# A two-layer transformer kernel: FFN result copied out of PSUM before it is normalized, recurrence weights loaded early, and the router run one chunk ahead of the shared expert

## The chip, the cores and the metric

The kernel runs on one core of a Trainium2 chip. The metric is the device time of one execution in microseconds. TensorE (PE in the profile) multiplies, VectorE (DVE), ScalarE (ACT) and GpSimd (POOL) do the elementwise work, SyncE (SP) issues most transfers. All engines execute their own instruction lists strictly in order and wait for each other on counting semaphores.

## The reference, cut to what matters

Two layers on 2048 tokens of width 512, each an attention-like part and an FFN part, with a layer norm ahead of each part and a residual around it.

```python
x = x + attention(ln(x))
x = x + fp4_ffn(ln(x))        # h = silu(gate) * up ; y = h @ w_down.T ; y / rms(y)
x = x + recurrence(ln(x))     # state = d*state + (1-d)*(x @ W_in.T) ; state @ W_out.T + bias
x = x + moe(ln(x))            # softmax router, top 6 of 64 experts, at most 128 tokens each,
                              # plus a shared expert (gs * us) @ sh_down.T of inner width 704
```

## The kernel before, in words

The 16 token tiles of 128 tokens live in SBUF as `x_residual` for the whole kernel. Work goes in four chunks of 512 tokens (four tiles each). Six phases follow each other, with a barrier of all engines between two of them; the change touches three: `ffn_phase`, `recurrence_phase` and `router_phase`. Every product is made of high and low float parts, so each operand is split (a copy that rounds, `..._hi`, on ScalarE, and a subtraction, `..._lo`, on VectorE or GpSimd) and `product3` (lines 215 to 225) issues three matmuls per term. The order of work on every engine is written out by hand; nothing is reordered.

**FFN.** A chunk has 11 groups g. For each group TensorE makes eight products of two matmuls in a ring of four PSUM banks (`gate_sum`, `gate_rest`, `hidden` are where ScalarE, line 1111, and VectorE, line 1158, scale and add them up), and 12 matmuls of the down product (`down`), which gathers in banks 4 to 7 over all 11 groups. `downs_of` says after which group's products a down runs: none after g = 2, two after g = 4. GpSimd adds `gate_rest` to `gate_sum` (line 1052) and makes `hidden_lo` (line 1043). When a chunk's down is complete, ScalarE squares it out of PSUM (`square_y`, line 1123) at g = 2 of the next chunk, VectorE makes a first guess of the inverse root (`guess_rms`), GpSimd refines it in twelve small operations (`gpsimd_refine`), and VectorE, at g = 3, adds the scaled result to the residual (`add_y`, line 1170). The layer norm of the next chunk is interleaved: statistics at g = 4, `gpsimd_rstd` (another twelve small GpSimd operations) at g = 4, normalizing (line 188) at g = 5 and 6, transposes from g = 7. After the last chunk the same chain runs with nothing beside it, and `w_in_raw` is loaded after the last gate and up product.

**Recurrence.** Splits `w_in` and `w_out` (`w_out_lo` is one long GpSimd operation, line 1258), projects in, scans with VectorE (line 1351), projects out. In chunk c = 0, between two scans, VectorE makes the low parts of chunk 1 (`ln_xt_lo`, line 211), for which `project_in(1)` on TensorE waits, and normalizes the tiles of chunk 2, for which it waits for GpSimd's second `gpsimd_rstd`.

**Router and shared expert.** For each chunk: `logits_of`, `turn_logits` (line 1548), softmax and `choose` on VectorE (top 6; lines 1663 to 1683), `turn_keys` (line 1554), and the shared expert in six groups of 24 matmuls, whose products VectorE multiplies (`sh_hidden`, line 1729) and GpSimd splits (line 1530); TensorE starts group n only when `sh_hidden` of group n - 2 is there. Then four tiles of the shared down product and `add_y` (line 1704). `rank` (lines 1695 and 1697) keeps, for each expert, its first 128 tokens: 16 rounds a chunk on VectorE, in any order with the rest, but chunk after chunk. GpSimd, before all this, splits the shared weights; the last of them, `sh_down_lo` (line 1522), waits for ScalarE's `sh_down_hi` (line 1637), and that for a transfer.

## Time and profile before

| what | value |
|---|---|
| median of 3 runs | 1881.22 us (1876.69 to 1886.66) |
| the profiled execution's own time | 1878.89 us |
| its span | 1877.0 us |
| TensorE busy | 1693.2 us (90%) |
| VectorE busy | 1097.0 us |
| ScalarE busy | 697.1 us |
| GpSimd busy | 623.2 us |
| mean granted TensorE clock | 0.957 of full |

The span is the time from the first to the last instruction of the profiled execution, the own time lies 1.9 us above it. Busy times add up over the whole span; matmuls are pipelined, so "busy" includes time in which TensorE is paced by others. A row of the timeline gives the start in us, the duration, the engine, the line of the kernel, the operation, output and inputs, how many were merged, and in square brackets how long the engine sat idle before it and what ended that.

### The profile page before, as it was taken

The page shows a single profiled execution, that of the slowest core. Times are in us where ns is not written, and L with a number is a line of the kernel's source. Part 1 is how long each engine was busy: PE and PEld are TensorE (multiplying, and loading weights), DVE is VectorE, ACT ScalarE, POOL GpSimd, SP SyncE. Part 2 cuts the span into 40 slices and gives each one's busy share as a digit, 9 for nine tenths or more (in the row PEclk, how much of TensorE's full clock was granted, in tenths as well). Part 3 has the DMA queues.
Part 4 walks back from the last instruction along what each step waited for, and adds up shares of the span by engine and source line. Part 5 has one row for each costly group of instructions (what it writes and reads, how often), then busy time and mean ns, then how long its engine had stood idle before and what let it go on. Part 6 is the DMA issues. An engine that isn't in the chain of part 4 may idle for free. (4 is left out here: it accounts for less than half of the span.)

```text
span 1877.0 us, 22599 instructions
## 1 busy us (share of the span) xinstructions
PE 1693.2 (90%) x7201; PEld 1184.8 (63%) x7201; DVE 1097.0 (58%) x2379; ACT 697.1 (37%) x1316; POOL 623.2 (33%) x862
## 2 busy tenths in 40 slices
PE   6997999999997998898958999999799999999995
PEld 5885555555456666676746767676576666666663
DVE  5444766766635767666768567788544444444442
ACT  3120555555532453444432242212133333333332
POOL 3001433333640334333354141111223444334432
PEclk9997899999998999998978999999899999999998
DMA  7236356665423200000030021112699999999994
GB/s 249 105 123 184 100 150 170 177 167 156 110 61 131 116 1 1 1 1 1 1 110 1 0 69 48 46 40 105 213 338 339 330 316 342 329 333 333 338 331 105
DMA packets 120661, 284.80 MB, mean 152 GB/s; under 512 B 23457, under 2 KB 35233, under 8 KB 120289
## 3 DMA queue, kind: packets, MB, share of 16 engines
q1 hardware_dynamic: 106208, 247.71, 38.7%
q0 software_dynamic: 14336, 35.66, 9.0%
q8 instruction: 59, 0.97, 0.2%
q14 instruction: 58, 0.47, 0.1%
HBM read 224.03 MB, written 54.69 MB: 148 GB/s over the span
## 5 line engine op out<-in xcount | busy, mean ns | idle before, releaser
L1826 POOL DMA_INDIRECT out_x<-e_y,row_out x64 | 144.1, 2252 | 310.8 <-DVE row_out L1908 176.2
L830 ACT ACTIVATE probs<-bank 128x512 f32<-128x512 f32 (+3 forms) x384 | 167.8, 501 | 191.0 <-PE bank L778 189.3
L1096 PE MATMUL bank<-ln_xt_hi,gu_codes 128*128 128x512 f32 x352 | 151.3, 430 | 36.6 <-ACT gate_sum L1111 15.0
L753 PE MATMUL bank<-k_stack,q_stack 96*128 96x512 f32 (+3 forms) x384 | 148.4, 408 | 26.5 <-DMA k_stack<-qk_parts 14.6
L1861 PE MATMUL bank<-w_gate,xgt 128*128 128x352 f32 x512 | 163.6, 463 | 0.0
L1861 PE MATMUL bank<-w_up,xgt 128*128 128x352 f32 x512 | 161.9, 459 | 0.0
L873 DVE CUSTOM_DVE_ANT_0 masked_scores<-bank,wide_mask 128x128 bf16<-128x128 f32 (+3 forms) x256 | 116.3, 483 | 56.8 <-PE bank L753 55.9
L702 POOL TENSOR_SCALAR_AFFINE_SELECT probs<-probs 128x128 f32<-128x128 f32 x256 | 79.1, 325 | 201.2 <-ACT probs L830 197.3
L1908 DVE COPY row_out<-slot_rows 128x1 uint32<-128x1 uint32 x64 | 9.8, 152 | 228.5 <-DMA out_x<-e_y,row_out 228.5
L1097 PE MATMUL bank<-ln_xt_lo,gu_codes 128*128 128x512 f32 x352 | 143.2, 407 | 0.0
L778 PE MATMUL bank<-q_stack,k_stack 98*128 98x512 f32 (+3 forms) x384 | 141.5, 383 | 1.9 <-ACT probs L830 1.8
L792 PE MATMUL bank<-probs,v_ones 128*64 128x512 f32 (+3 forms) x768 | 142.3, 507 | 0.0
L1861 PEld LDWEIGHTS bank<-w_up,xgt 128*128 128x128 f32 x512 | 97.3, 190 | 54.2
L1861 PEld LDWEIGHTS bank<-w_gate,xgt 128*128 128x128 f32 x512 | 93.8, 193 | 41.4 <-issue 1.3
L1096 PEld LDWEIGHTS bank<-ln_xt_hi,gu_codes 128*128 128x128 f32 x352 | 68.3, 194 | 81.6 <-ACT gate_sum L1111 20.7
L753 PEld LDWEIGHTS bank<-k_stack,q_stack 96*128 96x128 f32 x384 | 77.1, 202 | 64.7 <-DVE max_parts L873 18.4
L1931 DVE TENSOR_TENSOR e_down_lo<-w_down,e_down_hi 128x1024 fp32r<-128x1024 f32 (+1 forms) x128 | 116.2, 950 | 0.0
L1158 DVE SCALAR_TENSOR_TENSOR hidden<-bank,gu_scale,hidden 128x512 f32<-128x512 f32 x132 | 99.1, 751 | 15.8 <-ACT hidden L1111 5.1
L877 DVE TENSOR_REDUCE max_parts<-bank 128x1 f32<-128x512 f32 x128 | 82.5, 683 | 41.9 <-PE bank L753 41.8
L778 PEld LDWEIGHTS bank<-q_stack,k_stack 98*128 98x128 f32 x384 | 73.6, 193 | 52.2 <-ACT probs L830 24.9
L1879 ACT ACTIVATE e_y<-bank,xg 128x512 f32<-128x512 f32 x64 | 44.0, 688 | 162.6 <-PE bank L224 162.6
L1889 ACT ACTIVATE e_down_hi<-w_down 128x1024 fp32r<-128x1024 f32 (+1 forms) x128 | 100.0, 832 | 0.0
(242 smaller groups left out, 3817.5 us busy)
## 6 DMA issues: line engine op xcount, KB each, us to landing
w_gate<-in_w_gate SPq DMA_DIRECT2D x64, 704.0 KB, 6.7
w_up<-in_w_up SPq DMA_DIRECT2D x64, 704.0 KB, 8.4
w_down<-in_w_down SPq DMA_DIRECT2D x64, 512.0 KB, 9.0
q_stack<-qk_parts SPq DMA_DIRECT2D x96, 128.0 KB, 4.0
k_stack<-qk_parts SPq DMA_DIRECT2D x96, 128.0 KB, 4.1
w_down<-in_w_down SPq DMA_DIRECT2D x64, 192.0 KB, 9.7
qk_parts<-qk_stage_hi SPq DMA_DIRECT2D x32, 256.0 KB, 2.0
qk_parts<-qk_stage_lo SPq DMA_DIRECT2D x32, 256.0 KB, 2.3
```

The lines of the kernel that those rows point to most:

```text
L753: pe.matmul(m.bank[MAXB[at % 3]][:, 0:cols], qs[slot][j][0:ROWS, q * P:(q + 1) * P], ks[slot][j][0:ROWS, half * CH:half * CH + cols], star ...
L778: pe.matmul(bank[:, 0:cols], ks[slot][j][0:ROWS + 2, k * P:(k + 1) * P], qs[slot][j][0:ROWS + 2, q0:q0 + cols], start=True, stop=True).the ...
L792: pe.matmul(m.bank[OUTB[c]][j * 2 * HD:(j + 1) * 2 * HD, q0 - c * CH:q0 - c * CH + cols], vs[p % 2][j][:, k, :], probs[u % PROBS][:, 0:col ...
L830: act.activation(probs[u % PROBS][:, 0:cols], m.bank[EXPB[u % 3]][:, 0:cols], ACT.Exp, scale=scale).then_inc(exp_ready, 1)
L873: dve.tensor_tensor_reduce(out=masked[at % 4][:, 0:cols], in0=bank[:, 0:cols], in1=wide_mask[:, CH - cols:], scale=1.0, scalar=-3e38, op0= ...
L1096: pe.matmul(bank[:, :], gu[:, k, w], hi[:, k, :], start=True, stop=False)
L1097: pe.matmul(bank[:, :], gu[:, k, w], lo[:, k, :], start=False, stop=True).then_inc(product_done, 1)
L1158: dve.scalar_tensor_tensor(out=total[:, :], in0=m.bank[RING[at % 4]][:, :], scalar=gu_scale[:, half * G0 + g, k:k + 1], in1=total[:, :], o ...
L1826: pool.indirect_dma_start(out=a["out"][:, :], out_offset=bass.IndirectOffsetOnAxis(ap=row_out[e % YS][:, :], axis=0), in_=y[e % YS][:, :], ...
L1861: last = pe.matmul(m.bank[bank[e % 2]][:, 0:F], xt[e % 2][:, k, :], w[e % R][:, k, :], start=(k == 0), stop=(k == KT - 1))
L1889: last = act.activation(down_hi[e % 2][p, k, :], w_down[e % R][p, k, :], ACT.Copy)
L1931: last = dve.tensor_tensor(down_lo[e % 2][p, k, :], w_down[e % R][p, k, :], down_hi[e % 2][p, k, :].bitcast(F32), ALU.subtract)
```

## The change

FFN: at g = 2 of the next chunk ScalarE copies the four PSUM banks of the down product to a new SBUF tile `y` (`copy_y`, between its reads of the ring), so that the next down may start: `downs_of` becomes one down after every group from g = 2. Squares are read from `y` at g = 3, the guess and GpSimd's refinement come at g = 4 (ahead of the layer norm's own refinement at g = 4), the additions at g = 5 and 6; the statistics move from g = 4 to g = 3. There are three instead of four `hidden_hi`/`hidden_lo` buffers. After the last chunk `y` is only copied; its squares, guess, refinement and additions go into the recurrence phase. `w_in_raw` is loaded in two halves behind the FFN weights.

Router: layer norm buffers are doubled. Statistics, refinement and normalizing of chunk c + 1 move to g = 0, the transposes to g = 2 to 5, and the logits, softmax and `choose` of chunk c + 1 between the down tiles of chunk c. `rank` rounds follow a table. The final transposing of the slots moves ahead of the last down tile.

```diff
@@ ffn_phase
-    SLOTS = 4
+    SLOTS = 3
+    m.w_in_raw = [Arena(nc, m.attention_rows).put("w_in_raw0", [P, KT // 2, D], F32)]
...
-        return {2: [], 3: [(c, 0)], 4: [(c, 1), (c, 2)]}.get(g, [(c, g - 2)])
+        return [(c, g - 2)]
...
-            sp.wait_ge(product_done, products)
-            sp.dma_start(m.w_in_raw[:, :, :], a["w_in"].rearrange("(k p) n -> p k n", p=P)).then_inc(w_in_loaded, 16)
+            for half, raw in enumerate(m.w_in_raw):
+                rows = slice(half * D // 2, (half + 1) * D // 2)
+                sp.dma_start(raw[:, :, :], a["w_in"][rows, :].rearrange("(k p) n -> p k n", p=P)).then_inc(w_in_loaded, 16)
...
-                    if c >= 1 and g == 2:
+                    if c >= 1 and g == 4:
                         pool.wait_ge(root.ready, c)
                         need(pool, y_added, TPC * (c - 1))
                         root.gpsimd_refine(pool, y_rms[:, :], rms_ready)
                     if g == 4:
                         ln.gpsimd_rstd(pool, c + 1)
             to_lo(G0 * NCH - 1)
-            pool.wait_ge(root.ready, NCH)
-            pool.wait_ge(y_added, TPC * (NCH - 1))
-            root.gpsimd_refine(pool, y_rms[:, :], rms_ready)
...
-                        need(pe, y_added, TPC * (c - 1) + j + 1)
+                        need(pe, y_copied, TPC * (c - 1) + j + 1)
...
+            def copy_y(c, j):
+                act.wait_ge(down_done, TPC * (G0 * c + G0 - 1) + j + 1)
+                need(act, y_added, TPC * (c - 1) + j + 1)
+                act.activation(y[:, j, :], m.bank[DOWNB[j]][:, :], ACT.Copy).then_inc(y_copied, 1)
...
                     read(c, g, GATE, 0, gate[n % 2])
+                    if c >= 1 and g == 2:
+                        copy_y(c - 1, 0)
+                        copy_y(c - 1, 1)
                     need(act, gate_ready, n - 1)
                     read(c, g, GATE, 2, gate_rest[n % 2])
+                    if c >= 1 and g == 2:
+                        copy_y(c - 1, 2)
+                        copy_y(c - 1, 3)
...
-                    if c >= 1 and g == 2:
+                    if c >= 1 and g == 3:
                         for j in range(TPC):
                             square_y(c - 1, j)
...
-                    if c >= 1 and g == 3:
-                        add_y(c - 1)
+                    if c >= 1 and g in (5, 6):
+                        add_y(c - 1, 2 * (g - 5))
                     add(c, g, GATE, 3, gate_rest[n % 2], 2)
-                    if g == 4:
+                    if g == 3:
                         if c + 1 == NCH:
                             dve.wait_ge(y_added, TPC)
                         ln.vector_stats(dve, c + 1)
...
-                    if c >= 1 and g == 2:
+                    if c >= 1 and g == 4:
                         guess_rms(c - 1)
...
-            guess_rms(NCH - 1)
-            add_y(NCH - 1)
+            for j in range(1, TPC, 2):
+                dve.wait_ge(down_done, TPC * (G0 * NCH - 1) + j + 1)
+                dve.wait_ge(y_added, TPC * (NCH - 2) + j + 1)
+                dve.tensor_copy(y[:, j, :], m.bank[DOWNB[j]][:, :]).then_inc(y_copied, 1)
@@ recurrence_phase
             ln.gpsimd_rstd(pool, 1)
+            pool.wait_ge(root.ready, 1)
+            root.gpsimd_refine(pool, y_rms[:, :], rms_ready)
             raw, hi, lo = parts["w_out"]
             pool.wait_ge(w_hi_ready["w_out"], 1)
             pool.tensor_tensor(lo[:, :, :], raw[:, :, :], hi[:, :, :].bitcast(F32), ALU.subtract).then_inc(w_ready["w_out"], 1)
...
+            for j in range(TPC):
+                need(act, squared, j)
+                act.activation(square[:, :], m.y_last[:, j, :], ACT.Square, accum_out=square_sum[:, j:j + 1]).then_inc(squared, 1)
...
             ln.vector_normalize(dve, 1)
             ln.vector_stats(dve, 2)
+            dve.wait_ge(squared, TPC)
+            root.vector_guess(dve, square_sum[:, :], 1.0 / D, RMS_EPS)
...
                     if c + 2 <= NCH:
                         ln.vector_normalize_tile(dve, c + 2, e)
+                    if c == 0:
+                        if e == 0:
+                            dve.wait_ge(rms_ready, 1)
+                        add_y(e)
@@ router_phase
+    RANKED = {(0, 5): 2, (1, 0): 3, (1, 1): 3}
+    RANKED.update({(c, g): n for c in (2, 3) for g, n in ((0, 1), (1, 2))})
+    RANKED.update({(c, g): 2 if c < 3 else 4 for c in (1, 2, 3) for g in range(2, GS)})
+    RANKED.update({(0, GS + j): 2 for j in range(TPC)})
+    RANKED.update({(c, GS + j): n for c in (1, 2) for j, n in enumerate((2, 1, 1, 1))})
... (GpSimd, behind the unchanged splits of the shared weights)
                     n = GS * c + g
+                    if g == 0 and c + 1 < NCH:
+                        ln.gpsimd_rstd(pool, c + 1)
                     pool.wait_ge(hidden_hi_ready, n + 1)
...
-                    if g == 2 and c + 1 < NCH:
-                        ln.gpsimd_rstd(pool, c + 1)
... (TensorE)
+                        if c == 0 and g == 3 and name == "sh_gate":
+                            turn_keys(c)
+                    if c == 0 and g == 0:
                         turn_logits(c)
-                    if g == 3:
+                    if c >= 1 and g == 1:
                         turn_keys(c)
+                    if g >= TURN_AT and c + 1 < NCH:
...
+                        ln.tensor_turn(pe, c + 1, g - TURN_AT)
...
+                    if j == 0 and c + 1 < NCH:
+                        logits_of(c + 1)
+                    if j == 1 and c + 1 < NCH:
+                        turn_logits(c + 1)
+                    if j == 2 and c + 1 == NCH:
+                        pe.wait_ge(rank_step, 2 * ROUNDS * NCH)
+                        pe.transpose(m.bank[EB][:, 0:E], kept[:, :], m.ident[0:E, 0:E]).then_inc(kept_turned, 1)
... (VectorE)
+            softmax_shift(0)
             for c in range(NCH):
-                softmax_shift(c)
                 for g in range(GS):
-                    if g == 2:
+                    if c == 0 and g == 2:
                         choose(c)
-                    if g == 3 and c + 1 < NCH:
+                    if g == 0 and c + 1 < NCH:
                         ln.vector_stats(dve, c + 1)
...
                     dve.tensor_tensor(hidden[n % 2][0:r, :], silu[n % 2][0:r, :], m.bank[UPB[n % 2]][0:r, :],
                                       ALU.mult).then_inc(hidden_ready, 1)
+                    if g == 0 and c + 1 < NCH:
+                        dve.wait_ge(xn_stored, 16 * (c + 2))
+                        ln.vector_normalize(dve, c + 1)
+                    if g > TURN_AT and c + 1 < NCH:
...
+                        ln.vector_lo(dve, c + 1, g - TURN_AT - 1)
+                    rank_some(c, g)
+                if c + 1 < NCH:
+                    ln.vector_lo(dve, c + 1, GS - TURN_AT - 1)
                 for j in range(TPC):
                     add_y(TPC * c + j)
+                    if j == 1 and c + 1 < NCH:
+                        softmax_shift(c + 1)
+                    if j == 2 and c + 1 < NCH:
+                        choose(c + 1)
+                    rank_some(c, GS + j)
```

## Rows read from the trace of the kernel before

**Rows 1.** The page's first line.

```profile
span 1877.0 us, 22599 instructions
```

**Rows 2.** FFN, router: length, busy PE, PEld, DVE, ACT, POOL, granted clock, DMA share, GB/s.

```profile
595.20:948.50 353.30, 322.71 (x1296) 239.82 (x1296) 237.73 (x362) 161.69 (x267) 131.71 (x172) 0.94 0.09 34
1089.00:1326.00 237.00, 227.98 (x980) 167.50 (x978) 181.49 (x381) 56.28 (x84) 51.14 (x64) 0.99 0.18 64
```

**Rows 3.** What TensorE waited for in the FFN: total us, times, longest.

```profile
PE bank L1096 <- ACT gate_sum L1111: 15.0, 12, 2.8
PE bank L1096 <- DVE gate_rest L1158: 10.7, 3, 3.9
```

**Rows 4.** Timeline of ScalarE in the FFN: first read of a group.

```profile
612.17 0.67 ACT L1111 ACTIVATE gate_sum<-bank,gu_scale 128x512 f32<-128x512 f32 x1
618.34 0.67 ACT L1111 ACTIVATE gate_sum<-bank,gu_scale 128x512 f32<-128x512 f32 x1
...
693.63 0.67 ACT L1111 ACTIVATE gate_sum<-bank,gu_scale 128x512 f32<-128x512 f32 x1
701.29 0.68 ACT L1111 ACTIVATE gate_sum<-bank,gu_scale 128x512 f32<-128x512 f32 x1
...
739.44 0.67 ACT L1111 ACTIVATE gate_sum<-bank,gu_scale 128x512 f32<-128x512 f32 x1
```

**Rows 5.** Timelines of three engines, from FFN end to the recurrence's first matmul.

```profile
953.47 0.75 DVE L1170 SCALAR_TENSOR_TENSOR x_residual<-bank,y_inverse_rms,x_residual 128x512 f32<-128x512 f32 x1 [3.40 <-POOL y_inverse_rms L127]
957.14 1.15 ACT L1302 ACTIVATE w_in_hi<-w_in_raw 128x512 fp32r<-128x512 f32 x2 [7.70 <-PEq L1952]
962.86 0.80 PE L222 MATMUL bank<-ln_xt_hi,w_in_hi 128*128 128x512 f32 x1 [14.44 <-DVE w_in_lo L1331]
```

**Rows 6.** Timelines of GpSimd, VectorE and TensorE in the recurrence's first chunk.

```profile
965.63 4.53 POOL L1258 TENSOR_TENSOR w_out_lo<-w_out_raw,w_out_hi 128x2048 fp32r<-128x2048 f32 x1
979.74 1.49 DVE L188 TENSOR_SCALAR ln_xn<-x_residual,ln_mean_var,ln_rstd 128x512 f32<-128x512 f32 x1 [0.66 <-POOL ln_rstd L127]
988.90 0.54 DVE L188 TENSOR_SCALAR ln_xn<-x_residual,ln_mean_var,ln_rstd 128x512 f32<-128x512 f32 x1
991.26 0.77 PE L222 MATMUL bank<-ln_xt_hi,w_in_hi 128*128 128x512 f32 x1 [6.46 <-issue]
```

**Rows 7.** Timelines of ScalarE, GpSimd and TensorE in the router's first chunk.

```profile
1100.35 2.35 ACT L1637 ACTIVATE sh_down_hi<-sh_stage 128x2560 fp32r<-128x2560 f32 x1 [1.49 <-DMA sh_stage<-in_sh_down]
1103.30 7.08 POOL L1522 TENSOR_TENSOR sh_down_lo<-sh_stage,sh_down_hi 128x2560 fp32r<-128x2560 f32 x2 [8.05 <-ACT sh_down_hi L1637]
1094.24 0.46 PE L1548 MATMUL bank<-ident,logits_e 64*128 64x64 f32 x4
1111.77 0.63 PE L1554 MATMUL bank<-ident,keys 128*64 128x128 f32 x4
```

**Rows 8.** Timeline of VectorE in the router's second chunk.

```profile
1163.45 0.40 DVE L1663 TENSOR_REDUCE exp_sum<-logits 128x4 f32<-128x256 f32 x1
...
1167.19 0.68 DVE L1729 TENSOR_TENSOR sh_hidden<-sh_silu,bank 128x512 f32<-128x512 f32 x1
...
1171.21 2.45 DVE L162 BATCH_NORM_STATS2 ln_stats<-x_residual 128x6 f32<-128x512 f32 x4
...
1175.10 0.81 DVE L1695 MAX8 kept<-ranks 64x8 f32<-64x640 f32 x1
...
1176.86 0.82 DVE L1695 MAX8 kept<-ranks 64x8 f32<-64x640 f32 x1
...
1179.17 1.90 DVE L188 TENSOR_SCALAR ln_xn<-x_residual,ln_mean_var,ln_rstd 128x512 f32<-128x512 f32 x4
```

**Rows 9.** What TensorE waited for in the router, and the router's end.

```profile
PE bank L222 <- DVE x_residual L1704: 3.1, 1, 3.1
PE bank L222 <- issue: 2.4, 2, 1.2
...
1325.74 0.67 DVE L1704 TENSOR_TENSOR x_residual<-bank,x_residual 128x512 f32<-128x512 f32 x1
```

More of the change, by code:

```diff
@@ L34 @@
 SBUF_END = 229344
+W_IN_AT = 174464
 class Memory:
@@ L974, in ffn_phase @@
     root = InverseRoot(nc, arena, "rms", TPC)
+    m.w_in_raw = [Arena(nc, m.attention_rows).put("w_in_raw0", [P, KT // 2, D], F32)]
+    assert arena.at <= W_IN_AT
+    arena = Arena(nc, W_IN_AT)
+    m.w_in_raw.append(arena.put("w_in_raw1", [P, KT // 2, D], F32))
     RING, DOWNB = (0, 1, 2, 3), (4, 5, 6, 7)
@@ L1012, in downs_of @@
             return [(c - 1, G0 - 2 + g)] if c else []
-        return {2: [], 3: [(c, 0)], 4: [(c, 1), (c, 2)]}.get(g, [(c, g - 2)])
-    m.w_in_raw = Arena(nc, m.base).put("w_in_raw", [P, KT, D], F32)
+        return [(c, g - 2)]
     w_in_loaded = s("w_in_loaded")
@@ L1145, in _ @@
             to_hi(G0 * NCH - 1)
-            for j in range(TPC):
-                square_y(NCH - 1, j)
+            for j in range(0, TPC, 2):
+                copy_y(NCH - 1, j)
         @block.vector
@@ L1214, in recurrence_phase @@
     st_lo = [arena.put(f"state_lo{i}", [P, KT, CH], F32R) for i in range(2)]
+    square = arena.put("y_last_square", [P, D], F32)
+    square_sum = arena.put("y_last_square_sum", [P, TPC], F32)
+    y_rms = arena.put("y_last_inverse_rms", [P, TPC], F32)
+    root = InverseRoot(nc, arena, "rms_last", TPC)
+    assert arena.at <= W_IN_AT
     INB, OUTB = (2, 3, 4), (5, 6, 7)
@@ L1440, in router_phase @@
     GATEB, UPB, DOWNB = (2, 3), (4, 5), (6, 7)
-    EB, TB = DOWNB
+    EB, TB = ln.banks
+    KEYB = [TB] + [EB] * (NCH - 1)
+    TURN_AT = 2
     SENTINEL = 2.0
     ROUNDS = CAP // 8
+    RANKED = {(0, 5): 2, (1, 0): 3, (1, 1): 3}
[3 more added lines that the diff above has]
+    RANKED.update({(c, GS + j): n for c in (1, 2) for j, n in enumerate((2, 1, 1, 1))})
+    assert sum(RANKED.values()) == NCH * ROUNDS
     s = nc.alloc_semaphore
@@ L1614, in hidden_to_hi, with copy_logits @@
                 act.activation(hidden_hi[0:r, g, :], hidden[n % 2][0:r, :], ACT.Copy).then_inc(hidden_hi_ready, 1)
-            for c in range(NCH):
+            def copy_logits(c):
                 act.wait_ge(logits_done, c + 1)
@@ L1631, in _ @@
                     act.activation(silu[n % 2][0:r, :], m.bank[GATEB[n % 2]][0:r, :], ACT.Silu).then_inc(silu_ready, 1)
+                    if c == 0 and g == 3:
+                        copy_keys(c)
                     if g >= 1:
@@ L1637, in _ @@
                             act.activation(down_hi[p, k, :], stage[p, k, :], ACT.Copy).then_inc(down_hi_ready, 1)
+                    if g >= TURN_AT and c + 1 < NCH:
+                        if c == 0 and g == TURN_AT:
+                            act.wait_ge(w_ready["sh_up"], 1)
+                            act.wait_ge(w_rest_ready["sh_up"], 1)
+                        ln.scalar_hi(act, c + 1, g - TURN_AT)
                 hidden_to_hi(c, GS - 1)
-                act.wait_ge(up_done, GS * (c + 1))
                 if c + 1 < NCH:
-                    for j in range(TPC):
-                        ln.scalar_hi(act, c + 1, j)
+                    copy_logits(c + 1)
+                    exponentials(c + 1)
         @block.vector
```

135 lines of the change are left out of this document (77 added, 58 removed).

## The prediction, made before the changed kernel was run

> **What bounds the kernel now.** I read the page for the span, 1877.0 us [rows 1], then the table by stretch, then for each stretch TensorE's waits, then the timelines of the other engines around these waits. The reader is to see first that both changed stretches are TensorE's: it is busy 322.7 of 353.3 us in the FFN and 228.0 of 237.0 us in the router [rows 2]. So the change can gain only what TensorE loses there, and loses whatever it makes TensorE wait. The experts' phase behind them starts from a barrier and is untouched; I take its length as fixed.
>
> The two stretches differ in how much there is to gain. In the FFN TensorE waited 15.0 us for ScalarE's first read and 10.7 us for VectorE's `gate_rest`, the latter in three pieces of up to 3.9 us, one for each chunk that has an earlier chunk's result to normalize [rows 3]. Around the router's chunk ends it waited once 3.1 us and twice 1.2 us [rows 9], and its clock stood at 0.99 [rows 2]. The router is nearly full: there is little to win and much to spoil.
>
> **A measure for the FFN group.** The first read of a group by ScalarE marks the group. From 612.17 to 618.34 there is no down, yet the group lasts 6.17 us [rows 4]: this is the readers' own cycle (ScalarE read, VectorE's adds, product, ScalarE's `hidden_hi`, next read). So what is put into that cycle lengthens the group one for one. In chunk 1 group 2 lasts 701.29 - 693.63 = 7.66 us, and groups 3 to 6 together 739.44 - 701.29 = 38.15 us [rows 4]; with g = 2 that is 45.8 us.
>
> **FFN, chunks 1 to 3, after the change.** Group 2: four copies instead of squares. No row has this copy; the nearest bound is from below 0.6 us (the reads take 0.67 to 0.68 with a scale [rows 4]) less overlap, so about 0.5 each, and 0.7 from above: 2.0 to 2.8, and I take the middle of the low half, with the cycle about 8.0 us. Group 3 gets the statistics: 1175.10 - 1171.21 less one product of 0.6 is 3.3 us [rows 8], so 6.2 + 3.3 = 9.5; before, this work lay beside two downs, now beside one, so TensorE idles some 2.6 us. The four squares on ScalarE hide behind these statistics on VectorE. Group 4 is TensorE's, 6.5 us. Group 5 is the costly one: GpSimd gets the rms refinement at g = 4 only after VectorE's guess at the end of the group, and the layer norm's refinement behind it. One refinement is 3.4 us (VectorE idle before its first addition [rows 5]), two are 6.8. Behind them on GpSimd's list are `hidden_lo` of g = 4 and the `gate_sum` addition of g = 5; for that addition wait Silu, the product, ScalarE's next read and then TensorE. From about 0.3 us before group 5 that makes 6.6, then 1.3 and 1.3 for GpSimd's two and 2.1 for Silu, product and `hidden_hi`: 11.4 us instead of 6.5. Group 6: two additions of 0.7 and two normalizings of 0.7 in VectorE's list: 6.2 + 2.8 = 9.0. Sum: 8.0 + 9.5 + 6.5 + 11.4 + 9.0 = 44.4, and 0.5 for a clock at its low level after the idle of g = 5: 44.9, a gain of 0.9 a chunk, 2.7 in three. The stall of before isn't removed; its work is spread over groups that have nothing to spare. In chunk 0 there is nothing to normalize and the down that is no longer skipped gains about 1.5. FFN loop: -4.2; bounds: +3 if the clock drops twice a chunk, -20 if the idle of g = 3 and 5 stays hidden.
>
> **FFN end.** Before, VectorE's additions start at 953.47, and the next phase at 957.14 [rows 5]. The last down ends 5.0 us before the first of these (3.4 of refinement, 0.6 of guess, 1.0 of a square), at 948.4. Now a copy of 0.7 and the same barrier of 0.95 follow: 950.2. That is -7.0. The transfer of `w_in_raw` was not what the phase waited for, and moves behind the FFN weights, where the DMA queues are all but empty (share 0.09 [rows 2]); that part is worth nothing.
>
> **Recurrence.** The seven microseconds come back here. GpSimd's list now has: refinement of chunk 1's norm, wait for VectorE's guess (behind chunk 1's normalizing and chunk 2's statistics), the rms refinement, `w_out_lo` of 4.53 us, and only then chunk 2's `gpsimd_rstd`. Before, `w_out_lo` ran at 965.63, hidden under VectorE's work, and the refinement was there at 979.7 [rows 6]. In times of before: VectorE's guess comes at 971.7 (its normalizing isn't stretched by `w_out_lo` any more, 1.9 us [rows 8] in place of six), 3.4 gives 975.2, 4.5 gives 979.7, 3.4 gives 983.1: chunk 2's first tile is 3.4 us late. Behind it on VectorE stand the scans and low parts of chunk 1, and now three additions of 0.7 to 1.4 ahead of the last of them, together 2.1 to 2.9. For that last one TensorE waits at 991.26 with 6.46 us of idle already [rows 6], and then it is full to the end of the chunk. So +5.5; bounds +3.5 and +9.
>
> One row shows why the additions may cost double: the same normalizing takes 1.49 us beside GpSimd's bias additions and 0.54 alone [rows 6]. The Trainium skill (GPSIMD Engine Reference, Specifications) says that GpSimd shares its SBUF interfaces with VectorE and contends with instructions that have two SBUF inputs; the rows agree for the one-input case that they show. The addition read PSUM before and reads SBUF twice now, so by that page all of them near GpSimd work would stretch; with all three at 1.4 the sum here would be +7 instead of +5.5.
>
> **Router.** Chunk 0: VectorE normalizes chunk 1 right behind `sh_hidden` of g = 0, at about 1099.5 (logits turned at 1094.7 [rows 7], shift 0.8, statistics 3.3, product 0.7), and stops there for GpSimd's refinement. That stands behind `sh_down_lo`, unchanged: ScalarE's `sh_down_hi` gets its transfer at 1100.35, GpSimd works from 1103.30 for 7.08 us [rows 7], to 1110.4; 3.4 of refinement, 1113.8; 2.0 to 2.8 of normalizing; then `sh_hidden` of g = 1, done at 1117.0. TensorE needs it for g = 3, which it reaches at 1111.77 less one group of 5.6 (three groups from 1094.24 to 1111.77 [rows 7]), 1106. So it waits 11 to 11.5 us, then restarts at the lower clock. What that costs is read from the router: a mean granted clock of 0.99 over 237.0 us [rows 2] is 2.4 us missing, with one long wait of 3.1 [rows 9]; I take 2. So +13.4.
> Chunk 1: from its logits on VectorE has four additions and two products (3.6), 11 rounds of `rank` of 1.76 each [rows 8] (19.4), shift 0.8, `choose` 3.7 [rows 8], statistics 3.3, 2.9 of waiting for the refinement, normalizing 1.9, and some 3.2 of waiting for tiles: 38.8. TensorE, at 5.6 / 24 = 0.23 a matmul, has logits 2.8, three down tiles of 4.6 (18 matmuls and the gaps at a shorter operand), and g = 0 to 2 with turns, 18: 35. It waits 4.0, and again 2 for the clock: +6. Other small waits for the logits' norm: +1.2; the transposes, 0.6 for four [rows 7], stood between down tiles where a gap hid part of them: +2.
> Chunk 3: 16 rounds in four groups are 7.05 us a group against 5.6, so `sh_hidden` of g = 5 is 6.4 us late and the first down tile waits 1.6 and 4.1 us, 2 for the clock: +7.7. In return goes what was lost before: 3.1 with 2 of clock, twice 1.2 [rows 9], about 1.1 of smaller ones, and the last rounds that held back the final addition at 1325.74, 2.3: -10.9, and 1.8 for tiles that TensorE makes at a closer pace. Sum: 13.4 + 6 + 1.2 + 2 + 7.7 - 10.9 - 1.8 = +17.6. Bounds: +4 (no wait in chunk 0) and +26.
>
> **Sum.** -4.2 - 7.0 + 5.5 + 17.6 = +11.9 us. Against the profiled execution's own time of 1878.9 that is 1890.8; the median of the runs shown is 2.3 higher, so 1893, 0.63% slower.
>
> **Rivals.**
> *The FFN's chunk ends come back whole* (faster, the other side). Before, each costs TensorE up to 2.8 us behind ScalarE and a third of 10.7 behind VectorE [rows 3], and about 2 of lower clock, 8 a chunk. If GpSimd's two refinements in g = 4 don't hold back TensorE, the FFN gives 24 instead of 2.7: -9.4, 1872. It decides if group 5 lasts under 8 us. For it: TensorE has four banks of slack; against it: the readers' cycle of 6.17 leaves only 0.4.
> *GpSimd isn't late in router chunk 0.* If the refinement comes with g = 1 done, 13.4 fall away: 1879.7. Against it: the order in the list and the row at 1103.30.
> *The low clock lasts longer and VectorE's backlog is carried on* into chunk 2: another 8 to 10, 1902.
> *The tail of chunk 3 hides:* `rank` late, but its first tile waits only 2 us: 1887.
>
> **Chances.** Forecast 0.50 (own range 1885 to 1901), whole chunk ends 0.15, GpSimd in time 0.12, longer low clock 0.14, hidden tail 0.09. 0.5% is 9.4 us, about what a measurement of this kernel can tell from no change: the borders are 1871.8 and 1890.6. The forecast lies close to the upper one and gives two thirds to slower, the rest to same; with the others: slower 0.49, same 0.36, faster 0.15. The range is 1871 to 1903: down to the first rival, up to the third.
>
> **What would show it.** Right: in the router's chunk 0 an idle of about 11 us on TensorE ahead of g = 3, ended by `sh_hidden`, and VectorE's normalizing waiting about 14 us for GpSimd; an FFN group 5 of 11 us, ended by the GpSimd addition of line 1052; the barrier after the FFN at about 2 us behind the last down; the recurrence's second projection some 5 us later after the barrier; in the last router chunk a down tile waiting for the last `sh_hidden_lo`. Wrong: FFN groups 2 to 6 of a chunk in under 40 us (45.8 before), or a router stretch of less than 245 us (237 before).

## The result, and the profile after

| | before | after |
|---|---|---|
| median | 1880.66 us (8 runs, 1872.79 to 1886.66) | 1894.34 us (8 runs, 1890.51 to 1900.14) |
| profiled execution, own time | 1878.89 us | 1898.8 us |
| mean granted TensorE clock | 0.957 | 0.954 |

The changed kernel takes 1.0075 of the time of the kernel before, 95% interval 1.0051 to 1.0099: slower by some 14 us, more than the half per cent that the prediction set as its border. The forecast was 1893 us.

The first line of the page, against [rows 1]:

```profile
span 1896.6 us, 22616 instructions
```

The table by stretch, against [rows 2]: the FFN to its last down, the router to its last addition, and six microseconds of the router behind its longest wait. Columns: length, busy PE, PEld, DVE, ACT, POOL, granted clock, DMA share, GB/s.

```profile
595.30:950.00 354.70, 328.42 (x1296) 239.73 (x1296) 243.24 (x363) 166.87 (x275) 133.51 (x172) 0.95 0.09 34
1086.80:1343.60 256.80, 235.26 (x993) 173.92 (x993) 177.05 (x385) 59.22 (x87) 51.30 (x64) 0.95 0.17 59
...
1118.00:1124.00 6.00, 5.99 (x19) 4.78 (x20) 3.69 (x21) 1.94 (x4) 1.40 (x1) 0.62 0.56 197
```

The FFN is a little longer than before although TensorE waits less in it, and the router is longer at a lower clock, 0.95 against 0.99. The third row shows what a wait leaves behind: the clock is granted at 0.62, a mixture of the low level of 1.2 GHz and the high one of 2.4, so six microseconds hold 3.7 us of full-rate work, a loss of 2.3. Over the six microseconds behind the waits of 4.3 and 3.8 us shown further down it is 0.62 and 0.58, a loss of 2.3 and 2.5.

What TensorE waited for in the FFN, against [rows 3] (total us, times, longest):

```profile
PE bank L1098 <- ACT gate_sum L1113: 12.2, 11, 1.3
...
PE bank L1098 <- DVE gate_rest L1171: 4.2, 3, 2.2
PE bank L1098 <- DVE hidden L1171: 4.1, 3, 1.5
```

The three long waits behind `gate_rest` are gone, 25.7 us have become 20.5, and yet nothing is gained. The measure by groups says why. ScalarE's first reads in chunk 1, groups 1 to 6, against [rows 4]:

```profile
695.72 0.67 ACT L1113 ACTIVATE gate_sum<-bank,gu_scale 128x512 f32<-128x512 f32 x1
...
703.43 0.67 ACT L1113 ACTIVATE gate_sum<-bank,gu_scale 128x512 f32<-128x512 f32 x1
...
712.62 0.67 ACT L1113 ACTIVATE gate_sum<-bank,gu_scale 128x512 f32<-128x512 f32 x1
719.21 0.69 ACT L1113 ACTIVATE gate_sum<-bank,gu_scale 128x512 f32<-128x512 f32 x1 [0.31 <-PE bank L1099]
...
732.38 0.67 ACT L1113 ACTIVATE gate_sum<-bank,gu_scale 128x512 f32<-128x512 f32 x1
...
741.42 0.67 ACT L1113 ACTIVATE gate_sum<-bank,gu_scale 128x512 f32<-128x512 f32 x1
```

The first row opens group 2. From it groups 2 to 6 last 7.7, 9.2, 6.6, 13.2 and 9.0 us, 45.7 in all, against 45.8 before. Group 5 alone holds 13.2. GpSimd's list across groups 4 and 5:

```profile
718.80 0.20 POOL L121 TENSOR_TENSOR rms_root_t<-rms_root_y 128x4 f32<-128x4 f32 x1 [2.64 <-DVE rms_root_y L109]
...
721.87 0.20 POOL L128 TENSOR_TENSOR y_inverse_rms<-rms_root_y,rms_root_t 128x4 f32<-128x4 f32 x1
...
725.89 0.20 POOL L128 TENSOR_TENSOR ln_rstd<-ln_root_y,ln_root_t 128x4 f32<-128x4 f32 x1
726.04 1.29 POOL L1048 TENSOR_TENSOR hidden_lo<-hidden,hidden_hi 128x512 fp32r<-128x512 f32 x1
```

It waits 2.64 us for VectorE's guess at the very end of group 4, works through both refinements from 718.8 to 726.0, and only then takes `hidden_lo` of g = 4 and the addition that all readers of group 5 wait for.

Recurrence, timelines of four engines, against [rows 5, 6]. They are the next phase's first split on ScalarE, GpSimd's `w_out_lo`, VectorE's first tile of chunk 2, the first two of the moved additions, and then, with the time starting over, TensorE's three starts behind a wait:

```profile
952.22 2.19 ACT L1328 ACTIVATE w_in_hi<-w_in_raw 128x512 fp32r<-128x512 f32 x4 [2.27 <-PEq L2044]
...
971.03 4.54 POOL L1284 TENSOR_TENSOR w_out_lo<-w_out_raw,w_out_hi 128x2048 fp32r<-128x2048 f32 x1
...
978.83 1.46 DVE L189 TENSOR_SCALAR ln_xn<-x_residual,ln_mean_var,ln_rstd 128x512 f32<-128x512 f32 x1 [8.37 <-POOL ln_rstd L128]
980.21 1.75 DVE L1378 SCALAR_TENSOR_TENSOR x_residual<-y_rows,y_last_inverse_rms,x_residual 128x512 f32<-128x512 f32 x1
...
986.15 0.74 DVE L1378 SCALAR_TENSOR_TENSOR x_residual<-y_rows,y_last_inverse_rms,x_residual 128x512 f32<-128x512 f32 x1
...
957.96 0.79 PE L223 MATMUL bank<-ln_xt_hi,w_in_hi 128*128 128x512 f32 x1 [7.93 <-DVE w_in_lo L1360]
984.88 1.09 PE L198 MATMUL bank<-ident,ln_xn 128*128 128x128 f32 x4 [11.65 <-DVE ln_xt_lo L212]
992.35 0.76 PE L223 MATMUL bank<-ln_xt_hi,w_in_hi 128*128 128x512 f32 x1 [6.38 <-issue]
```

TensorE's idle ahead of the recurrence is 7.9 us instead of 14.4; but its start at 992.35 was at 991.26 before, so the gain is gone by then. GpSimd is late by its longer list, VectorE stands 8.4 us for it, and TensorE stands 11.7 behind VectorE.

Router, timelines of three engines, against [rows 7 to 9]:

```profile
1104.31 6.97 POOL L1581 TENSOR_TENSOR sh_down_lo<-sh_stage,sh_down_hi 128x2560 fp32r<-128x2560 f32 x2 [7.96 <-ACT sh_down_hi L1713]
...
1114.61 2.76 DVE L189 TENSOR_SCALAR ln_xn<-x_residual,ln_mean_var,ln_rstd 128x512 f32<-128x512 f32 x4 [14.01 <-POOL ln_rstd L128]
...
1116.05 1.11 PE L198 MATMUL bank<-ident,ln_xn 128*128 128x128 f32 x4 [8.88 <-DVE ln_xn L189]
1118.01 0.80 PE L223 MATMUL bank<-ln_xt_hi,sh_gate_hi 128*128 128x512 f32 x1 [0.85 <-DVE sh_hidden L1823]
...
1182.85 0.79 PE L223 MATMUL bank<-ln_xt_hi,sh_gate_hi 128*128 128x512 f32 x1 [4.34 <-DVE sh_hidden L1823]
...
1318.27 0.50 PE L223 MATMUL bank<-sh_down_hi,sh_hidden_hi 128*128 128x512 f32 x1 [1.13 <-POOL sh_hidden_lo L1591]
1325.80 0.79 PE L223 MATMUL bank<-sh_down_hi,sh_hidden_hi 64*128 64x512 f32 x1 [3.77 <-POOL sh_hidden_lo L1591]
```

Read in order: `sh_down_lo`, VectorE's 14.0 us for GpSimd, TensorE's 8.9 and 0.9 us behind it in chunk 0, 4.3 in chunk 1, and 1.1 and 3.8 at the first down tile of chunk 3.

By stage, after against before: FFN from its first read to the first read of the last group 341.3 against 339.8 (+1.6); from there to the recurrence's first matmul 20.0 against 26.5 (-6.5); to the router's first matmul 128.8 against 122.8 (+6.0); to the experts' first `row_in` 260.1 against 244.0 (+16.1); the experts 549.7 against 547.2. The last difference isn't taken as a cost: that phase is not touched, and in the eleven profiles of the experiments below it lasts 539.6 to 555.4 us.

### The profile page after: what moved, and what is told of

Same layout as the page of the kernel before. It is cut to its first block and busy times, and to the rows that moved or that the text cites. A ratio compares the mean times of both kernels' runs of the same rounds, so it can differ in the third digit from the quotient of the medians.

```text
span 1896.6 us, 22616 instructions
## 1 busy us (share of the span) xinstructions
PE 1701.3 (90%) x7201; PEld 1188.7 (63%) x7201; DVE 1090.7 (58%) x2381; ACT 703.6 (37%) x1330; POOL 616.2 (32%) x862
## 5 line engine op out<-in xcount | busy, mean ns | idle before, releaser
L1918 POOL DMA_INDIRECT out_x<-e_y,row_out x64 | 135.2, 2112 | 319.4 <-DVE row_out L2000 210.0
L1098 PE MATMUL bank<-ln_xt_hi,gu_codes 128*128 128x512 f32 x352 | 156.1, 443 | 32.3 <-ACT gate_sum L1113 12.2
L1048 POOL TENSOR_TENSOR hidden_lo<-hidden,hidden_hi 128x512 fp32r<-128x512 f32 x44 | 56.7, 1290 | 136.5 <-ACT hidden_hi L1119 136.5
```

Source lines behind the costliest of these rows:

```text
L1098: pe.matmul(bank[:, :], gu[:, k, w], hi[:, k, :], start=True, stop=False)
L1918: pool.indirect_dma_start(out=a["out"][:, :], out_offset=bass.IndirectOffsetOnAxis(ap=row_out[e % YS][:, :], axis=0), in_=y[e % YS][:, :], ...
```

## The experiments

Each ratio is to the kernel before, from five rounds with both on one chip.

**One part alone.** e1 is the changed kernel with the whole `router_phase` of before, e2 the kernel before with the whole `router_phase` of the changed one.

> The FFN and recurrence parts of the change alone, the router as before. My theory: the FFN loop 1.6 us longer than before, the FFN's end 6.5 us shorter, the recurrence's first chunk 6 us longer, as in the trace of the changed kernel, so 1 us above before (ratio 1.000 to 1.002), and the router starts about 1 us later than before and lasts 237 us. Rival: the two parts interact (the recurrence with its extra GpSimd work leaves the router a different start), then the router stretch is longer than 240 us here too and the time lies 5 us or more above before.

> The router part of the change alone, FFN and recurrence as before. My theory: the whole loss is the router's. From the router's first matmul to the first row_in of the experts 16 us more than before (260 against 244), with TensorE idle 8.9 and 4.3 us behind VectorE in chunks 0 and 1 and 1.1 and 3.8 us in chunk 3; time 1.008 to 1.009 of before. Rival: half of the loss comes from the other parts or from the experts' stage behind; then the ratio is under 1.005.

Measured: 0.9983 (0.9959 to 1.0007) for FFN and recurrence, 1.0070 (1.0048 to 1.0091) for the router, which lasts 260.6 us with the same idles of 8.7, 0.9, 4.3, 1.1 and 3.8. In the first one the router lasts 245.8 us, 1.8 more than before; 1.6 of it stand in the stretch from its first matmul to the turned logits (10.7 us at a granted clock of 0.84, against 9.1 at 1.00), so the rival of an interaction finds little. The whole loss is the router's; the FFN and recurrence part is worth nothing measurable.

**GpSimd's list in the router's first chunk,** in three steps.

In e3 the refinement for chunk 1 goes ahead of the wait, and the loop makes only the later ones:

```diff
+            ln.gpsimd_rstd(pool, 1)
             pool.wait_ge(down_hi_ready, 2)
             for p, k in TILES:
...
-                    if g == 0 and c + 1 < NCH:
+                    if g == 0 and 1 <= c and c + 1 < NCH:
                         ln.gpsimd_rstd(pool, c + 1)
```

In e5 the block of `sh_down_lo` moves into the loop, behind `sh_hidden_lo` of g = 1; in e9 the same block stands under `g == 3`:

```diff
-            pool.wait_ge(down_hi_ready, 2)
-            for p, k in TILES:
...
                     if g == 0 and c + 1 < NCH:
                         ln.gpsimd_rstd(pool, c + 1)
+                    if c == 0 and g == 2:
+                        pool.wait_ge(down_hi_ready, 2)
+                        for p, k in TILES:
...
                     pool.wait_ge(hidden_hi_ready, n + 1)
```

> The changed kernel with one line moved: in the router GpSimd runs the twelve small operations of the refinement for chunk 1 before it waits for sh_down_hi and works 7 us on sh_down_lo. My theory: VectorE's normalizing and sh_hidden of g = 1 come about 11 us earlier, TensorE's idle ahead of g = 3 of chunk 0 (8.9 and 0.9 us and the low clock behind it) is gone, and the router is 10 to 13 us shorter: time 0.994 of the changed kernel, within 3 us of before. Rival one, it is VectorE's load that TensorE waits for: then it idles in chunk 1 or later for what chunk 0 gives, and less than 5 us are gained. Rival two, sh_down_lo now ends 3.4 us later and the first down tile waits for it: an idle of 1 to 3 us at the end of chunk 0.

Measured: 1.0046 (1.0027 to 1.0064), the router 257.3 us instead of 260.1. In this execution TensorE began the router at its low level: from its first matmul to the turned logits it took 11.7 us, in the changed kernel's profile 9.1. So the edit itself gave about 5.4 us, half of what I expected. The refinement is there at 1104.2, but TensorE still stands 4.7 us, for a reason that neither my theory nor the two rivals had. GpSimd, VectorE and TensorE around it:

```profile
1104.97 5.88 POOL L1582 TENSOR_TENSOR sh_down_lo<-sh_stage,sh_down_hi 128x2560 fp32r<-128x2560 f32 x1 [0.74 <-ACT sh_down_hi L1714]
...
1105.26 5.87 DVE L189 TENSOR_SCALAR ln_xn<-x_residual,ln_mean_var,ln_rstd 128x512 f32<-128x512 f32 x1
...
1111.05 1.50 DVE L189 TENSOR_SCALAR ln_xn<-x_residual,ln_mean_var,ln_rstd 128x512 f32<-128x512 f32 x1
...
1113.20 0.79 PE L223 MATMUL bank<-ln_xt_hi,sh_gate_hi 128*128 128x512 f32 x1 [4.71 <-DVE sh_hidden L1824]
```

One normalizing of 0.5 us takes 5.87 and ends 0.3 us behind GpSimd's operation of 5.88; the next takes 1.5 beside GpSimd's second, shorter operation. By these rows VectorE isn't slowed down in proportion, it is held until GpSimd's instruction is over. The Trainium skill (SBUF — State Buffer, section "SBUF: two separate sides") says that a pair of ports is shared under an exclusive lock: of a GpSimd instruction and a VectorE instruction that uses both ports for one tensor, or has two inputs in SBUF, the one that starts first holds the pair for its whole length and the other waits. The lengths agree here and in the rows below; which mode the normalizing ran in no trace shows.

> The changed kernel with the order of GpSimd's list in the router's first chunk changed: the refinement for chunk 1 first, then sh_hidden_lo of g = 0 and 1, and only then the 7 us of sh_down_lo. In the run that moved the refinement alone, the four normalizings of VectorE lay beside sh_down_lo and took 8.2 us instead of 1.9, so TensorE still stood 4.7 us. My theory: without a long GpSimd operation beside them they take 1.9 to 2.8 us, sh_hidden of g = 1 is there before TensorE wants g = 3, and neither the idle nor the low clock behind it is left: chunk 0 is 10 to 11 us shorter than in the changed kernel, 5 to 6 shorter than in the run before, ratio to before 1.002. Rival: the slow operations of VectorE are not due to sh_down_lo, and stay at 2 us each with TensorE idle over 3 us at the same place.

Measured: 1.0051 (1.0031 to 1.0071) where 1.002 was expected, no better than e3. The four normalizings take 1.92 us as expected and TensorE's idle ahead of g = 3 is 0.6. But the block hits what now lies beside it, the small operations that make `keys`:

```profile
1112.46 5.59 POOL L1587 TENSOR_TENSOR sh_down_lo<-sh_stage,sh_down_hi 128x2560 fp32r<-128x2560 f32 x1
...
1112.95 5.15 DVE L1764 TENSOR_SCALAR keys<-marked,key_of_token 128x64 f32<-128x64 f32 x1
...
1119.66 1.06 PE L1612 MATMUL bank<-ident,keys 128*64 128x128 f32 x4 [6.18 <-DVE keys L1764]
```

An operation on 64 elements of each partition that takes 0.25 us alone stands 5.15. The cost has nothing to do with its own size. TensorE's idle is moved to `turn_keys`, 6.2 us of it. My theory named the right cause and put the block on the wrong neighbour.

> The changed kernel with sh_down_lo one group later still on GpSimd's list: behind sh_hidden_lo of g = 2. Behind g = 1 it lay beside the four small operations of VectorE that make keys (0.7 us, then 6.7), and TensorE stood 6.2 us at turn_keys. My theory: what slows VectorE is an operation that reads and writes SBUF alone while GpSimd works on a long one; from g = 3 on VectorE has products and low parts with an input in PSUM, which the rows show at their usual 0.7 us beside GpSimd. So neither the normalizing nor keys is stretched, no idle over 1 us stands in chunk 0, and the router is 11 to 13 us shorter than in the changed kernel: ratio to before 1.001 to 1.002. Rival: every VectorE operation beside sh_down_lo is slowed; then sh_hidden and ln_xt_lo of g = 3 take 1.5 us and more and TensorE stands 1 to 4 us at g = 4 or 5.

Measured: 0.9992 (0.9968 to 1.0015), the router 249.9 us, 10.2 less than in the changed kernel where 11 to 13 were expected:

```profile
1111.48 7.07 POOL L1587 TENSOR_TENSOR sh_down_lo<-sh_stage,sh_down_hi 128x2560 fp32r<-128x2560 f32 x2
...
1111.91 0.69 DVE L1824 TENSOR_TENSOR sh_hidden<-sh_silu,bank 128x512 f32<-128x512 f32 x1 [3.00 <-issue]
1118.58 0.69 DVE L212 TENSOR_TENSOR ln_xt_lo<-bank,ln_xt_hi 128x512 fp32r<-128x512 f32 x1 [5.98 <-POOL sh_down_lo L1587]
...
1119.41 0.63 PE L198 MATMUL bank<-ident,ln_xn 128*128 128x128 f32 x4 [1.54 <-DVE ln_xt_lo L212]
```

`sh_hidden`, with one input in PSUM, takes its usual 0.69 us in the middle of `sh_down_lo`, so the rival falls. `ln_xt_lo` doesn't test it: it starts when `sh_down_lo` is over. What is left is 1.5 us on TensorE: `ln_xt_lo` waited by its semaphore for `sh_down_lo`, since it writes where the raw weights lay.

**The FFN's refinements.**

```diff
-                    if c >= 1 and g == 4:
-                        pool.wait_ge(root.ready, c)
-                        need(pool, y_added, TPC * (c - 1))
-                        root.gpsimd_refine(pool, y_rms[:, :], rms_ready)
                     if g == 4:
                         ln.gpsimd_rstd(pool, c + 1)
+                    if c >= 1 and g == 5:
+                        pool.wait_ge(root.ready, c)
+                        need(pool, y_added, TPC * (c - 1))
+                        root.gpsimd_refine(pool, y_rms[:, :], rms_ready)
...
-                    if c >= 1 and g in (5, 6):
-                        add_y(c - 1, 2 * (g - 5))
+                    if c >= 1 and g in (6, 7):
+                        add_y(c - 1, 2 * (g - 6))
```

> The changed kernel with GpSimd's two refinements of the FFN taken apart: the layer norm's at g = 4 at once, the rms one at g = 5 behind the gate addition, and the additions to the residual at g = 6 and 7 instead of 5 and 6. My theory: the wait of GpSimd for VectorE's guess with two refinements behind it is what makes group 5 last 11 to 13 us; group 5 falls to 8 to 9 (two normalizings and one refinement in the cycle), groups 2 to 7 of a chunk gain 3 to 5 us, the FFN 9 to 14 us in three chunks, ratio to before 1.000 to 1.003. Rival: the cycle of the readers has no slack anywhere, so 3.4 us of refinement only move from group 5 to 6 and the FFN gains less than 3 us.

Measured: 1.0015 (0.9995 to 1.0035). ScalarE's first reads of groups 5 to 7 in chunk 1:

```profile
718.73 0.69 ACT L1113 ACTIVATE gate_sum<-bank,gu_scale 128x512 f32<-128x512 f32 x1 [0.32 <-PE bank L1099]
...
726.73 0.67 ACT L1113 ACTIVATE gate_sum<-bank,gu_scale 128x512 f32<-128x512 f32 x1
...
735.78 0.67 ACT L1113 ACTIVATE gate_sum<-bank,gu_scale 128x512 f32<-128x512 f32 x1
```

Group 5 lasts 8.0 us in place of 13.2; in chunks 2 and 3 8.1 and 7.5 in place of 12.1 and 11.3. Group 6 stays at 9.1, group 7 becomes 8.1 instead of 7.0. Groups 2 to 7 of the three chunks sum to 146.0 us instead of 158.3: 12.3 us less with the same work in another order, 2.0 of it in group 4, which varies by itself (below). It isn't the luck of one profile: the four with this order (e6, e8, e10, e11) have 144.9 to 149.1 us there, the seven with the changed kernel's order 157.7 to 158.8. The rival, that the refinement only moves, falls.

**The rank rounds.** Same 64 rounds, another table; each row of the new one is a chunk, ten places from g = 0 to the fourth down tile.

```diff
-    RANKED = {(0, 5): 2, (1, 0): 3, (1, 1): 3}
-    RANKED.update({(c, g): n for c in (2, 3) for g, n in ((0, 1), (1, 2))})
-    RANKED.update({(c, g): 2 if c < 3 else 4 for c in (1, 2, 3) for g in range(2, GS)})
-    RANKED.update({(0, GS + j): 2 for j in range(TPC)})
-    RANKED.update({(c, GS + j): n for c in (1, 2) for j, n in enumerate((2, 1, 1, 1))})
+    ROUNDS_AT = ((0, 0, 0, 0, 2, 2, 2, 2, 1, 2), (1, 2, 2, 2, 2, 2, 2, 1, 1, 2),
+                 (1, 2, 2, 2, 2, 2, 2, 1, 1, 2), (3, 2, 3, 3, 3, 3, 2, 0, 0, 0))
```

> The changed kernel with another table of rank rounds: three or four fewer before g = 3 of chunk 1, two in a group instead of up to four, and chunk 3 begins its rounds at g = 1. My theory: VectorE's 1.76 us rounds are what sh_hidden is late by in chunks 1 and 3. The idle of 4.3 us in chunk 1 and those of 1.1 and 3.8 us in chunk 3 fall under 1 us in sum, and the router is 8 to 11 us shorter: ratio to before 1.002 to 1.003. The stall of chunk 0 stays as it is. Rival: the rounds only move the waits (to g = 4 and 5 of chunk 1, or to the kept turn at the end, which waits for the last round), and less than 4 us are gained.

Measured: 0.9996 (0.9970 to 1.0021), better than expected: the router takes 247.2 us, 13 less, although TensorE began it at its low level; that cost 1.3 us here (10.4 us to the turned logits at a granted clock of 0.86, against 9.1 at 1.00). TensorE's waits there, with none in chunks 1 to 3 over 0.6 us:

```profile
PE bank L198 <- DVE ln_xn L189: 8.7, 1, 8.7
...
PE bank L223 <- DVE sh_hidden L1821: 0.9, 1, 0.9
```

The idles that went sum to 9.2 us (4.3, 1.1 and 3.8); the rest, some 5 us, fits the 2.3 and 2.5 us of low clock behind the two long ones. The rival is refuted.

**Together.** e8 has the edits of e5, e6 and e7; e10 those of e9, e6 and e7.

> The changed kernel with the three edits at once: sh_down_lo later, GpSimd's refinements in the FFN taken apart, and the other table of rank rounds. If the three losses are separate, their gains add: 10 + 11 + 9 = 30 us under the changed kernel, 1865 us, ratio to before 0.991 to 0.993. If the second and third shrink because TensorE is bound at its full rate in the router (244 us from its first matmul to row_in before, with 4 us of waits), the sum ends nearer to 20 us and 0.997.

Measured: 0.9930 (0.9904 to 0.9955), 1866.1 us. The single edits had gained 0.24, 0.60 and 0.79% on the changed kernel, which would make 0.991: they add within the interval. My 30 us had counted on 10 from the first, which gave less than half.

> The kernel with all three edits (ratio 0.993) with sh_down_lo behind g = 2 instead of g = 1. My theory: its last large idle in the router, 5.8 us at turn_keys, and the low clock behind it go: 7 to 8 us less, ratio to before 0.989. Rival: VectorE's backlog shows at the next place (the first down tile, or g = 3 of chunk 1) and less than 3 us are gained, 0.992.

Measured: 0.9883 (0.9845 to 0.9921, from six runs of it), 1859.5 us, as expected and 21 us under the kernel before. The router takes 236.8 us against 244.0.

**The recurrence.** e4 changes the order in the changed kernel; e11 starts from e10.

On GpSimd e4 has the order `w_out_lo`, second layer norm refinement, rms refinement, and on VectorE the four additions together:

```diff
             ln.gpsimd_rstd(pool, 1)
-            pool.wait_ge(root.ready, 1)
-            root.gpsimd_refine(pool, y_rms[:, :], rms_ready)
...
                 if c + 2 <= NCH:
                     ln.gpsimd_rstd(pool, c + 2)
+                if c == 0:
+                    pool.wait_ge(root.ready, 1)
+                    root.gpsimd_refine(pool, y_rms[:, :], rms_ready)
...
-                    if c == 0:
-                        if e == 0:
-                            dve.wait_ge(rms_ready, 1)
-                        add_y(e)
...
                 if c == 0:
+                    dve.wait_ge(rms_ready, 1)
+                    for j in range(TPC):
+                        add_y(j)
                     dve.wait_ge(y_added, TPC)
```

e11 keeps the rms refinement first and moves `w_out_lo` behind `ln.gpsimd_rstd(pool, 2)`.

> The changed kernel with the recurrence's order mended: GpSimd runs w_out_lo and the second layer norm refinement before the rms refinement of the FFN's last chunk, and VectorE makes the four additions of that chunk behind the loop of scans of c = 0 instead of between them. My theory: the two waits (GpSimd's refinement late, additions ahead of the last low part) are what the recurrence lost; the idle behind ln_xt_lo falls from 11.7 to about 6 us, and the recurrence is 5 to 6 us shorter: time 0.997 of the changed kernel. Rival: the additions only move, and TensorE or ScalarE waits for them at the end of chunk 0 where x_residual is read next; then less than 2 us are gained and a new idle of 2 to 3 us stands at the start of the recurrence's second chunk.

Measured: 1.0058 (1.0035 to 1.0080), the recurrence 127.6 us instead of 128.8. TensorE's starts behind a wait:

```profile
984.09 0.76 PE L223 MATMUL bank<-ln_xt_hi,w_in_hi 128*128 128x512 f32 x1 [7.30 <-issue]
1001.53 0.63 PE L198 MATMUL bank<-ident,ln_xn 128*128 128x128 f32 x4 [2.88 <-DVE ln_xt_lo L212]
```

Counted from the recurrence's first matmul, the second projection starts 7.0 us earlier than in the changed kernel, more than I had hoped, and a new idle of 2.9 us stands in the next chunk, as the rival said. Behind it 3.7 of the 7.0 us are left, and 2.5 behind the low clock that follows. The last 1.3 are no effect of the edit that I can show: both kernels have a wait of 3.3 us later in the phase, and over the ten microseconds behind it the granted clock was 0.69 in e4 and 0.83 in the changed kernel's profile, but also 0.70 in e10, whose recurrence is the changed one. VectorE is nearly full from here on (22.6 of 25 us between 985 and 1010 in the changed kernel's profile, 22.3 before), so I read it that its four additions, 3 us, cost their time wherever they stand; no run without them tests that.

> The kernel before it, and in the recurrence w_out_lo (4.5 us on GpSimd) moved behind the second layer norm refinement, for which VectorE stood 8.4 us idle in the changed kernel. My theory: VectorE starts on the first tile of chunk 2 some 4.5 us earlier, but three or four of its SBUF operations now lie beside w_out_lo and take 1.5 to 2 us each instead of 0.5 to 1.2, so 1 to 3 us are left as a gain in the recurrence. Rival one: contention costs all of it (0 or a loss). Rival two: it costs nothing and 4 to 5 us are gained.

Measured: 0.9879 (0.9840 to 0.9917), the same as e10. The recurrence takes 128.5 us, against 128.8 in the changed kernel and 130.2 in e10, which has the same recurrence; those two differ by the clock behind the wait of 3.3 us.

```profile
959.12 4.49 POOL L1288 TENSOR_TENSOR w_out_lo<-w_out_raw,w_out_hi 128x2048 fp32r<-128x2048 f32 x1
...
959.21 4.69 DVE L189 TENSOR_SCALAR ln_xn<-x_residual,ln_mean_var,ln_rstd 128x512 f32<-128x512 f32 x1 [3.90 <-POOL ln_rstd L128]
...
968.49 1.09 PE L198 MATMUL bank<-ident,ln_xn 128*128 128x128 f32 x4 [10.40 <-DVE ln_xt_lo L212]
```

VectorE's wait for GpSimd shrinks from 8.4 to 3.9 us, and its first operation then stands 4.69 us beside `w_out_lo` instead of 1.46. Wait and operation together go from 9.8 to 8.6 us: most of the wait is still there under another name, the semaphore's before, the length of an instruction now. TensorE's idle shrinks by as much, from 11.7 to 10.4, but the next one grows from 6.4 to 7.3, and the second projection starts 34.1 us behind the phase's first matmul instead of 34.4. The first rival was right in the main: 0.3 us are gained where 1 to 3 were expected.

## Why the prediction was right, point by point

The forecast, 1893 us and slower, came out (1894.3). That it is within 1.3 us is partly luck. Its sum was +11.9 us; by the same stages the profile has +17.2 (1.6 - 6.5 + 6.0 + 16.1), and the execution that was profiled lies 4.5 us above the median of its eight. The medians differ by 13.7.

**Router: right.** Forecast +17.6, measured +16.1, and with both parts where they were put. Chunk 0: TensorE idle 9.7 us and turning for 1.1, between 1107.2 and 1118.0, with 2.3 of clock behind it, 12 where the sum had 13.4; VectorE waiting 14.0 for GpSimd, as named. Chunk 1: 4.3 where the sum had 4.0. Chunk 3: 1.1 and 3.8 where it had 1.6 and 4.1. e9 and e7 show the causes: the list order on GpSimd is worth 10.2 us, the rounds 13 or more. The price of the clock, 2 us for each long wait, was right too: 2.3, 2.3 and 2.5. The price hangs on the execution, though: over the six microseconds behind the same wait of 4.3 us the granted clock was 0.72 in e2, a loss of 1.7.

**FFN end and recurrence: right.** -7.0 forecast and -6.5 measured, +5.5 and +6.0. Of the moved additions one took 1.75 us beside GpSimd and the others 0.74, so the second case weighed there, all of them at 1.4, did not come. The row that was put beside it, normalizing at 1.49, is of an operation with one input; this one of 1.75 is the case with two inputs in SBUF. What e4 and e11 add is that another order returns little of the loss, 2.5 and 0.3 us; that the rest is VectorE's time for the additions is argued and not shown.

**FFN loop: the mechanism right, the size off.** The term was -4.2 and measured +1.6; in the seven profiles with this FFN it lasts 336.1 to 341.4 us, 339.2 on average, -0.7 against the 339.8 before. In chunks 1 to 3 I had -2.7; groups 2 to 6 sum to 137.2 us against 137.8, so -0.6. Group 5, sized at 11.4 (its parts as given, 6.8 - 0.3 + 1.3 + 1.3 + 2.1, make 11.2), took 13.2, 12.1 and 11.3, and group 4, sized at 6.5, took 6.6, 8.2 and 8.1. Group 2, 3 and 6 came in at 7.7, 9.2 and 9.0 for my 8.0, 9.5 and 9.0. e6 shows that group 5 is indeed GpSimd's two refinements.

Group 4 goes either way between executions of the same code, and the granted clock (third figure from the end) goes with it. Chunks 1 and 2 of the changed kernel's profile:

```profile
712.60:719.20 6.60, 5.75 (x24) 4.37 (x25) 4.78 (x9) 3.22 (x6) 2.89 (x4) 1.00 0.00 0
800.10:808.30 8.20, 7.35 (x24) 5.61 (x25) 4.77 (x9) 3.24 (x7) 3.67 (x8) 0.79 0.00 0
```

Both have the same idle of 1.3 us on TensorE at the start. In the eleven profiles with one or the other of the new FFN orders there are 33 such groups: ten took 6.6 us, all at 1.00, and twenty-three took 7.7 to 8.2, all at 0.78 or 0.79. So group 4 was mis-sized by the clock, which the prediction had not charged there. In the changed kernel's order group 5 takes some of it back: it lasts 12.7 to 13.2 us behind a group of 6.6 and 11.3 to 12.5 behind a slow one.

Chunk 0 was to give -1.5 and shows +2.1, and that is no effect of the change that I can show. From its first read to that of chunk 1 it took 83.7 us before; the changed FFN in eleven profiles took 81.1 to 85.8, the FFN of before once more 82.8. The granted clock goes with it: 81.1 us came with a granted clock of 0.98 over the chunk and 85.8 with 0.92; at 0.95 the changed FFN took 82.6 to 84.3, and that of before at 0.94 82.8 and 83.7. A gain of 1.5 us can't be seen in this.

**The rivals.** The FFN's chunk ends did not come back whole: group 5 was over 8 us. The border that was set doesn't carry the rival's price, though. e6 brings group 5 to 8.0, 8.1 and 7.5 by the order of GpSimd's list alone, and in the four profiles with that order the FFN lasts 328.2 us on average, 11.6 less than before and half of the 24 that the rival counted. GpSimd was late in router chunk 0. The low clock took 2.3 to 2.5 us over the six microseconds behind each long wait, and chunk 3's tail did not hide.

## What to carry to other kernels

When work is moved earlier, follow the list of the engine that has to serve it: here two moves of a small GpSimd refinement behind a long GpSimd operation or a late wait cost some 10 us each, and reordering that list and VectorE's rounds, with all the same work, turned 0.75% slower into 1.2% faster. A long GpSimd operation on SBUF is a hazard for VectorE as well as for its own list: put it beside VectorE work of the kinds that the next section shows at their usual length, or beside idle time, and check the neighbours after each move. Count an engine's load in each window before filling it: VectorE's rounds cost 13 us where six stood in the first two groups of chunk 1 and four in each later group of chunk 3.

## What the hardware showed that was not expected

- Some VectorE operations that meet a running GpSimd operation on SBUF stand until that one ends, whatever their own size: 5.87, 5.15 and 4.69 us for operations of 0.54, 0.25 and 0.54 us alone, beside GpSimd operations of 5.88, 5.59 and 4.49. Normalizing and `keys` (one tensor of SBUF to SBUF), the additions from `y` (0.74 alone, 1.75) and the scans (1.21 alone, 2.28) show it. Others keep their length: `sh_hidden`, which reads PSUM (0.69), the rank operations beside `sh_hidden_lo` (0.80 to 0.82), and the layer norm's statistics beside the addition of `gate_rest` (0.68 within 1.30), although the last two work on SBUF alone. In the profile the held ones look like slow VectorE instructions, not like a wait.
- It goes the other way too. In the changed kernel's profile one of GpSimd's small operations of 0.20 us, at 968.07 in the recurrence, took 0.99, until the scan that VectorE had begun at 967.84 ended at 969.07.
- The same code starts a phase at either clock level. After the same 3.0 us of idle the router's first matmul took 0.45 us in six of the thirteen profiles and 0.69 in seven. The stretch to the turned logits took 9.1 us in five of them, 10.4 to 10.7 in six and 11.7 or 11.8 in two, at granted clocks of 1.00, about 0.85 and about 0.76. Differences of 3 us between single profiles are within this.
